# Folding wv and wo into one matrix, ordering the first loads by use, and running attention tiles across the two sequences

## The reference

```python
# 1: causal attention, one head of 128
q = rope(xn @ wq);  k = rope(xn @ wk);  v = xn @ wv
s = (q * 128**-0.5) @ (k * 128**-0.5).T - 1e30 * (i < j)
o = softmax(s) @ v
x = x + o @ wo
# 2: x = x + ffn(layernorm(x))           token shift, sigmoid gate, squared relu
# 3: x = x + linear_attention(layernorm(x))   16 heads of 64, a state per head, gated
# 4: x = x + ffn(layernorm(x))           the same weights as block 2
```

## Time and profile before

| | us |
|---|---|
| median of 3 runs | 904.65 (904.13 to 906.27) |
| the profiled execution | 908.08, its span 906.0 |
| busy PE / DVE / ACT / POOL over the span | 824.8 / 554.9 / 569.4 / 584.4 |

### The profile page before, as it was taken

How to read it: one execution, slowest core, us unless ns; L and a number is a source line. 1 busy time by engine, 2 the same in 40 slices (tenths; PEclk the granted TensorE clock), 3 DMA queues, 4 the chain that set the end, 5 groups by cost and what they waited for, 6 DMA issues and landing times.

```text
span 906.0 us, 31429 instructions
## 1 busy us (share of the span) xinstructions
PE 824.8 (91%) x13280; PEld 711.7 (79%) x13280; DVE 554.9 (61%) x1296; ACT 569.4 (63%) x1202; POOL 584.4 (65%) x514
## 2 busy tenths in 40 slices
PE   4858998999797799999999999999999999997877
PEld 3647997899695687888788788888888888885776
DVE  3976566567684356557467467467467467566473
ACT  4746554665565666767767767767767766754544
POOL 4983211320455788977977977977977977986322
PEclk9988999999997899999999999999999999997999
DMA  5001000100100000000000000000000000000011
GB/s 190 26 12 36 25 13 1 31 18 2 25 1 1 1 3 3 4 3 3 3 3 3 4 3 3 4 3 3 4 2 3 3 3 3 3 3 2 13 31 51
DMA packets 19417, 12.38 MB, mean 14 GB/s; under 512 B 7760, under 2 KB 18768, under 8 KB 19024
## 3 DMA queue, kind: packets, MB, share of 16 engines
q1 hardware_dynamic: 19280, 10.39, 4.0%
HBM read 8.29 MB, written 2.10 MB: 11 GB/s over the span
## 4 chain that ended last, share of the span: by engine, by line
PE 50%; DVE 9%; POOL 4%; issue 3%; ACT 2%; DVEq 0%; POOLq 0%; ACTq 0%
PE la_ps L1465 7%; PE la_ps L1467 6%; PE la_ps L1466 6%; DVE la_u_lo L1773 4%; PE la_o_ps L1528 4%; PE la_o_ps L1544 4%; PE la_s_ps L1558 4%; PE la_ps L1575 3%; PE la_ps L1509 3%; DVE la_u L1767 3%; PE la_ps L1609 2%; PE la_ps L1496 2%; PE la_ps L1610 2%; PE la_ps L1611 2%; PE la_ps L1598 1%
## 5 line engine op out<-in xcount | busy, mean ns | idle before, releaser
L2109 POOL TENSOR_TENSOR la_coef<-la_ssk,lt_mhalf 128x32 f32<-128x32 f32 x16 | 87.1, 5442 | 71.2 <-DVE la_ssk L1784 71.2
L1465 PE MATMUL la_ps<-la_x_hi,w_hi 128*128 128x256 f32 x384 | 116.7, 304 | 2.0 <-ACT la_v L1924 1.0
L1467 PE MATMUL la_ps<-la_x_hi,w_lo 128*128 128x256 f32 x384 | 107.6, 280 | 0.1
L1466 PE MATMUL la_ps<-la_x_lo,w_hi 128*128 128x256 f32 x384 | 107.5, 280 | 0.0
L2141 POOL TENSOR_TENSOR la_scale<-la_scale,lt_mhalf 128x32 f32<-128x32 f32 x16 | 99.9, 6241 | 6.7 <-DVE la_scale L1760 6.4
L1807 DVE TENSOR_TENSOR lt_state<-la_s_ps,la_faded 128x512 f32<-128x512 f32 x62 | 42.6, 687 | 70.6 <-PE la_o_ps L1544 57.5
L1465 PEld LDWEIGHTS la_ps<-la_x_hi,w_hi 128*128 128x128 f32 x384 | 72.4, 189 | 14.5 <-issue 6.2
L713 ACT ACTIVATE at_probs<-at_s_ps,at_ntop 128x512 f32<-128x512 f32 (+2 forms) x80 | 49.0, 623 | 46.5 <-DVE at_ntop L655 46.4
L598 PE MATMUL at_o_ps<-V,at_probsT 128*128 128x128 f32 x544 | 74.6, 277 | 3.2 <-DVE at_probsT L507 2.0
L531 POOL CAST at_q_hi<-qk_hi 128x128 fp32r<-128x128 f32 x32 | 9.4, 294 | 104.9 <-PE at_s_ps L572 102.4
L598 PEld LDWEIGHTS at_o_ps<-V,at_probsT 128*128 128x128 f32 x544 | 69.1, 192 | 6.5 <-ACT at_probsT L729 2.3
(11 more groups left out here) (216 smaller groups left out, 2501.3 us busy)
## 6 DMA issues: line engine op xcount, KB each, us to landing
at_w_raw<-in_w SPq DMA_DIRECT2D x20, 128.0 KB, 2.2
X<-in_x SPq DMA_DIRECT2D x8, 256.0 KB, 2.9
out<-X SPq DMA_DIRECT2D x8, 256.0 KB, 2.3
qkv_cos<-in_cos SPq DMA_DIRECT2D x1, 1024.0 KB, 5.0
qkv_sin<-in_sin SPq DMA_DIRECT2D x1, 1024.0 KB, 7.2
lt_w_out<-in_w_out SPq DMA_DIRECT2D x4, 128.0 KB, 2.7
const<-in_const SPq DMA_DIRECT2D x1, 320.5 KB, 3.3
qkv_w<-in_w_qkv SPq DMA_DIRECT2D x1, 320.0 KB, 3.9
```

Of the source, the lines that this page charges most:

```text
L1465: eng.matmul(out, l_hi, r_hi, start=True, stop=False)
L1466: eng.matmul(out, l_hi, r_lo, start=False, stop=False)
L1467: return eng.matmul(out, l_lo, r_hi, start=False, stop=True)
L2109: eng.tensor_tensor(coef[:, :], ssk[:, :], mhalf[:, :], ALU.pow).then_inc(s["coef_step"], 1)
```

## The change

It has three parts. First, `qkv_phase` loads wo, turns wv on TensorE, copies it, multiplies it by wo and copies the product `w_vo`, which then takes wv's place in `values`; attention loses `scale_o`, `turn_o`, `copy_oT` and `project_o`, and `residual` becomes one operation on VectorE that scales o out of PSUM by the inverse row sum and adds X. The ring of PSUM banks holds only probabilities. Second, the loads of the beginning stand in order of use: the constants are cut into the identity (early) and the rest (last), and the cosine and sine tables come in four pieces, each waited for by `products`; preparation of the FFN weights moves behind tile 4 of sequence 0. Third, the scores, maxima and exponentials of sequence 1's first tiles are issued in the iteration of sequence 0's last tile, and the waits count tiles on across the sequences.

```diff
...
+        wo = sb("wo", [P, P])
+        wvT = sb("wvT", [P, P])
+        w_vo = sb("w_vo", [P, P])
...
                 if k == 0:
-                    eng.dma_start(const[:, :], io["const"]).then_inc(loaded_const, 16)
                     eng.dma_start(w[:, :, :], io["w_qkv"]).then_inc(loaded_w, 16)
+                    eng.dma_start(ident, io["const"][:, C_IDENT:C_IDENT + P]).then_inc(loaded_ident, 16)
+                    eng.dma_start(wo[:, :], io["wo"]).then_inc(loaded_wo, 16)
 
                 eng.wait_ge(loaded_x, 16 * (k + 1))
-                if k == 1:
-                    eng.dma_start(cos[:, :], io["cos"]).then_inc(loaded_rope, 16)
-                    eng.dma_start(sin[:, :], io["sin"]).then_inc(loaded_rope, 16)
+                if g.b == 1:
+                    part = slice(g.n * G, (g.n + 1) * G)
+                    if g.n > 0:
+                        eng.wait_ge(loaded_rope, 32 * g.n)
+                    eng.dma_start(cos[:, part], io["cos"][:, part]).then_inc(loaded_rope, 16)
+                    eng.dma_start(sin[:, part], io["sin"][:, part]).then_inc(loaded_rope, 16)
+            eng.dma_start(const[:, P:], io["const"][:, P:]).then_inc(loaded_rest, 16)
+            eng.wait_ge(loaded_rest, 16)
...
             def products(g, r):
                 if late(g, 1):
                     eng.wait_ge(rot_ready[r], g.count(1))
+                eng.wait_ge(loaded_rope, 32 * (g.n + 1))
...
             moments(Tile(0, 1))
-            eng.wait_ge(loaded_rope, 32)
+            eng.wait_ge(wv_turned, 1)
+            eng.tensor_copy(wvT[:, :], pr_ps[0][:, 0:P]).then_inc(wvT_ready, 1)
+            eng.wait_ge(w_vo_full, 1)
+            eng.tensor_copy(w_vo[:, :], pr_ps[1][:, 0:P]).then_inc(w_vo_ready, 1)
             run_slots(eng, slot)
...
         @block.tensor
         def _(eng):
-            eng.wait_ge(loaded_const, 16)
+            eng.wait_ge(loaded_ident, 16)
             eng.wait_ge(loaded_w, 16)
+            eng.transpose(pr_ps[0][:, 0:P], w[:, 4, :], ident).then_inc(wv_turned, 1)
+            eng.wait_ge(loaded_wo, 16)
+            eng.wait_ge(wvT_ready, 1)
+            eng.matmul(pr_ps[1][:, 0:P], wvT[:, :], wo[:, :], start=True, stop=True).then_inc(w_vo_full, 1)
...
-                    mm = eng.matmul(v_ps[g.b][:, j * P:(j + 1) * P], xT[:, g.b, j * P:(j + 1) * P], w[:, 4, :], start=True, stop=True)
+                    mm = eng.matmul(v_ps[g.b][:, j * P:(j + 1) * P], xT[:, g.b, j * P:(j + 1) * P], w_vo[:, :], start=True, stop=True)
...
-        def ahead(n):
+        def ahead(b, n):
 
             if n + 2 < SMALL:
-                return n + 2
-            return n + 1 if SMALL <= n + 1 < NT else None
+                return [(b, n + 2)]
+            if n + 1 == NT and b + 1 < B:
+                return [(b + 1, 0), (b + 1, 1)]
+            return [(b, n + 1)] if SMALL <= n + 1 < NT else []
...
-        jobs = []
-        for n in range(NT + 2):
-            if n < NT:
-                jobs += [("probs", n, j) for j in range(blocks(n))]
-            if 1 <= n <= NT:
-                jobs.append(("oT", n - 1, 0))
-            if n >= 2:
-                jobs.append(("wo", n - 2, 0))
+        jobs = [("probs", n, j) for n in range(NT) for j in range(blocks(n))]
...
-            def turn_o(b, n):
-                eng.wait_ge(o_ready, b * NT + n + 1 + CREDIT)
-                bank, full = wait_bank(b, ("oT", n, 0))
-                eng.transpose(bank[:, 0:P], o_n[:, n % 2, :], ident).then_inc(full, 1)
-
-            def project_o(b, n):
...
-                eng.matmul(bank[:, 0:P], oT[:, n % 2, :], wo[:, :], start=True, stop=True).then_inc(full, 1)
-
+            scores(0, 0)
+            scores(0, 1)
             for b in range(B):
-                scores(b, 0)
-                scores(b, 1)
-                for n in range(NT + 2):
-                    last = blocks(n) if n < NT else 0
+                for n in range(NT):
+                    last = blocks(n)
                     for j in range(min(last, 2)):
                         transposes(b, n, j)
-                    if ahead(n) is not None:
-                        scores(b, ahead(n))
-                    for j in range(last - 1):
+                    for later in ahead(b, n):
+                        scores(*later)
+                    for j in range(last):
                         values(b, n, j)
                         if j + 2 < last:
                             transposes(b, n, j + 2)
-                    if 1 <= n <= NT:
-                        turn_o(b, n - 1)
-                    if n >= 2:
-                        project_o(b, n - 2)
-                    if n < NT:
-                        values(b, n, last - 1)
...
             def residual(b, n):
-                k, before = ring(b, ("wo", n, 0))
-                eng.wait_ge(t_full[k], before + 1)
-                xt = X[:, bass.ds(b * NT + n, 1), :]
-                eng.tensor_tensor(xt, t_ps[k][:, 0:P].rearrange("p (t c) -> p t c", t=1), xt, ALU.add).then_inc(t_read[k], 1)
+
+                N = b * NT + n
+                eng.wait_ge(o_full, N + 1)
+                eng.wait_ge(total_step, 2 * N + 2)
+                xt = X[:, b * NT + n, :]
+                eng.scalar_tensor_tensor(xt, o_ps[n % 2][:, 0:P], total[:, n % 2, 1:2], xt, ALU.mult, ALU.add).then_inc(o_read, 1)
...
+                for n in range(NT):
+                    if n > 0:
+                        residual(b, n - 1)
+                    elif b > 0:
+                        residual(b - 1, NT - 1)
+                    if n + 2 < SMALL:
                         sum_rows(b, n)
-                    if ahead(n) is not None:
-                        maxima(b, ahead(n))
-                    if n < NT and ahead(n) != n + 2:
+                    for later in ahead(b, n):
+                        maxima(*later)
+                    if n + 2 >= SMALL:
                         sum_rows(b, n)
-                    for j in range(2, last):
+                    for j in range(2, blocks(n)):
                         copy_probs(eng, eng.tensor_copy, b, n, j)
-                    if 1 <= n <= NT:
-                        copy_oT(b, n - 1)
-                    if n >= 2:
-                        residual(b, n - 2)
+                    if b == 0 and n == GT:
+                        ffn_weights.vector(eng)
...
-            def scale_o(b, n):
-                N = b * NT + n
...
-                eng.activation(o_n[:, n % 2, :], o_ps[n % 2][:, 0:P], ACT.Copy, scale=total[:, n % 2, 1:2]).then_inc(o_ready, 1)
-
             eng.sem_inc(exp_ready, CREDIT)
-            eng.sem_inc(o_ready, CREDIT)
-            ffn_weights.scalar(eng)
+            exponentials(0, 0)
...
                     if n + 1 < NT:
                         exponentials(b, n + 1)
-                    scale_o(b, n)
+                    elif b + 1 < B:
+                        exponentials(b + 1, 0)
+                    if b == 0 and n == GT:
+                        ffn_weights.scalar(eng)
             tables.scalar_rates(eng)
```

68 lines of the change are left out of this document (23 added, 45 removed).

## The result

The changed kernel takes 884.07 us (median of 4 runs, 882.93 to 884.72), the kernel before in the same series 905.46 (904.13 to 909.5). The ratio is 0.9738, with a 95% interval of 0.9709 to 0.9767. The forecast was 884.4. The profiled executions took 882.93 and 908.08 us, with spans of 880.8 and 906.0.

The account below looks back on a forecast made before the run. TensorE was taken to bound mid-sequence attention, chains of waits the opening, sequence step and end. Terms summed to 20.3 us off 908.08, giving 887.8, less 3.43 to the median: 884.4 us, own range 880 to 888.5, overall 879.5 to 892.

Parts of the forecast that it names:

- The opening: Kernel's start up to the first products: they come earlier because the wait for the sine table goes; 3.5 us, bounds 0 and 4.7.
- the three chains: Opening, paths to the first products: third X lands near 10.9, products possible at 13.9; weights' product and TensorE, 14.5; VectorE's second copy, hidden.
- The start: Start of attention: the first mask no longer waits behind the FFN weights' preparation; 1.7 us, up to 2.0.
- The -0.3: Tile 4 of sequence 0: cost of the FFN weights' six instructions moved there; -0.3 us, bounds 0 and -1.1.
- my two readings of the clock: Start of attention: full clock returns at a fixed moment, gain 1.0 us, or earlier work brings it earlier, gain 2.0 us.
- TensorE's work on o, and the ring: Attention tiles: turn and wo product removed, 8.2 us, bounds 5 and 9.5; PSUM banks no longer wait for o's copies, 1.3.
- the first rival: Small attention tiles: VectorE and ScalarE take over, TensorE's saving pays only in tiles 9 to 15; 892.9 us, chance 0.13.
- Between the sequences: Step from sequence 0 to 1: the next sequence's first scores and exponentials lie under the last tile; 3.2 us, bounds 1.5 and 3.9.
- the end: End of attention: last values, projection and residual behind VectorE's FFN groups get shorter; 2.7 us, bounds 1.5 and 3.2.
- The opening gave more than nothing: Second rival, opening: it gives nothing because GpSimd and VectorE are full or a load is late again; 887.9 us, chance 0.10.
- The loads one behind another: Third rival, opening: SP's waits between X and table pieces make the kernel slower; 907.4 us, chance 0.03.
- My sign of being wrong: Stages after attention: one changing its length by more than 2 us would count against the forecast.

Follow-up runs that it names:

- w_late: The changed kernel with the FFN weights' preparation in tile 12 of sequence 0 instead of tile 4; median 884.92 us, attention 0.38 us shorter.
- u_weights: The changed kernel with the FFN weights' preparation back at the head of VectorE's and ScalarE's streams; median 885.41 us, attention 0.40 us longer.
- the pair put back: The changed kernel with one turn and one 128x128 product more per tile on TensorE, into unread PSUM columns; median 894.39 us, attention 6.2 us longer.
- fold_only: The kernel before with only wv and wo multiplied on chip, no projection of o, and the residual in one operation; median 894.91 us, ratio 0.9873.
- loads_only: The kernel before with only the new order of the loads, without the product of the weights; median 903.53 us, ratio 0.996.

## Why the prediction was right, step by step

**The opening** (3.5; 3.0 at the first products, 3.9 at the first scores). Right in the main cause, the wait for the tables. Of the three chains the one through the product and TensorE was the last, as said: `products` wait 0.67 us for TensorE. The third X landed at 11.41, 0.5 later than worked out. It was issued at 7.32, behind 0.33 + 0.43 us in which SP issues the two pieces, where I had started from 6.7. (The prediction's second estimate, 3.8 us, is worked out from a fit to DMAs that GpSimd issues; SyncE issues these, and from its own issue this one took 4.1.) The products were 0.4 later than forecast, but not for that: I had left out group 0's values, which TensorE makes from 10.98 for 2.04 us ahead of group 1's turn and projections. Before, they lay in the wait for the tables (10.06 to 12.13). By the Trainium skill, "DMA: Bandwidth & Descriptors", section "Bandwidth", loads under 1 MiB are the worse ones; whole tables under the same waits were slower by 3.7 us, so here what is queued ahead of X decided. That the new product is nearly free holds only with the new loads: under the old ones it costs 3.1 us, which no part of the prediction had.

**The start** (1.7; 1.92). The first mask came as early as said, but this term was mis-sized: 1.7 - 0.3 = 1.4 was counted, and undoing the step costs 0.40 by the end of attention. The -0.3 was about right (`w_late` gives 0.38 back), so the 1.7 was worth 0.8. The full clock returned at 68.90 instead of 73.51, 4.6 us earlier, but not because the start of attention was freed: in `u_weights`, where TensorE again stands 2.46 us behind its first scores, it returned at 68.61. What moved with it is the fall to half clock, while TensorE stands behind its last projections: 63.27 before, 58.66 after, 58.37 in `u_weights`. Between fall and return lie 10.2 us in all three. So of my two readings of the clock the fixed moment is the one borne out for this step; it moved with the end of the stage before, not with the start of attention. The other reading, which I took from the Trainium skill, "TensorE: Matmul & The Clock Gate", section "Part 1: The HAM clock gate", that the earlier work brings the clock earlier, isn't borne out by this pair. How much of the missing 0.9 us is the clock's and how much other chains' in the small tiles was not separated.

**TensorE's work on o, and the ring** (8.2 + 1.3; with the weights 9.2 for the tiles, 9.47 measured). The sum came out right, the split was wrong, and its two errors offset each other: that is luck. I multiplied 23 tiles by 0.336 us and left out tile 8 alone. The leads of the masks say where it pays: tiles 4 to 8 give 5.72, 6.46, 7.27, 7.26, 8.50, which is 0.7 a tile, twice what TensorE works on o (with the fold alone it is 0.9 a tile, in both sequences); tiles 8 to 15 give 8.50, 8.51, 8.62, 8.73, 9.00, 9.28, 9.83, 10.06, 0.22 a tile. (The turns in the earlier trace rows are tile 8's, not tile 9's as I wrote.) What the gain is lost to in tile 9 is in TensorE's timelines, first before, then after: turns of eight blocks of tile 9, of the last two, and of the first eight of tile 10.

```profile
101.21 1.06 PE L584 MATMUL at_t_ps<-const,at_probs 128*128 128x128 f32 x8
...
104.92 0.38 PE L584 MATMUL at_t_ps<-const,at_probs 128*128 128x128 f32 x2
...
106.81 1.04 PE L584 MATMUL at_t_ps<-const,at_probs 128*128 128x128 f32 x8
```
```profile
92.21 1.32 PE L594 MATMUL at_t_ps<-const,at_probs 128*128 128x128 f32 x8
...
96.30 0.38 PE L594 MATMUL at_t_ps<-const,at_probs 128*128 128x128 f32 x2
...
97.90 1.04 PE L594 MATMUL at_t_ps<-const,at_probs 128*128 128x128 f32 x8
```

Before, 101.21 to 106.81 is 5.60 us; after, 92.21 to 97.90 is 5.69. The second part is shorter (1.89 to 1.60) by the work on o that left. The first part is longer (3.71 to 4.09), of which 0.26 are the turns, which now last 1.32 instead of 1.06. ScalarE's timeline after shows why: the second exponential of tile 9 is still running when the turns have begun, and ends at 92.73.

```profile
92.05 0.68 ACT L699 ACTIVATE at_probs<-at_s_ps,at_ntop 128x512 f32<-128x512 f32 x1
```

So the probabilities of tile 9 come late as well. This is the first rival's mechanism, in tiles 8 and 9 instead of in all small tiles. TensorE counts as busy 48.00 of 48.02 us over it, since such a wait lies inside an instruction's length and in no idle.

In the small tiles it is the other way round: more than the work was saved. The fold took 15.4 us off attention. Of that TensorE's own time is 6.2 to 7.2 (the pair put back), ScalarE's 0.1, VectorE's 0.5. What is left, near 8, should be waits of the removed chain itself (values, scaling, turn, copy, projection, residual, and two more turns in the ring of banks), which no engine's time shows. Where it lies, `fold_only` set against the kernel before tells, by the masks and less what the pair costs in the same place: 2.5 us in tiles 0 to 8 of sequence 0, 1.6 in tiles 2 to 8 of sequence 1, 0.6 in tiles 8 to 15 of both, 1.8 from tile 15 of sequence 0 to tile 2 of sequence 1, 2.3 at the end, and 0.4 ahead of the first mask. These 9.2 us include what ScalarE and VectorE took. The trace shows one such wait named, 1.6 us in the earlier trace rows. That the rest is waits of this chain is reached by difference and was not tested, because a chain can't be put back without its work.

**Between the sequences** (3.2; 3.89) and **the end** (2.7; 2.70). Right. The step has two parts that I had not told apart: the run-on is worth 2.1 (1.9 without the scatter ahead of it), the fold 1.8 to 2.0. At the end VectorE holds to its own order as said, and the residual cost 0.35 instead of 0.29. TensorE's idle there fell from 1.99 to 1.60 us, where I had let it grow.

**The rivals.** VectorE and ScalarE taking over would have given 892.9: a pair of tiles, not the stretch, was due to them. The opening gave more than nothing. The loads one behind another never were late: no `products` waited for a table. My sign of being wrong, a later stage changed by more than 2 us, did show (3.3), but kernels with the change lie on both sides of it. The last step, from the profiled execution to the median (-3.43), held by luck: the profiled execution after lies 1.1 below its median, not 3.4 above. Between the profiled executions lie 25.2 us where I said 20.3; the later stages' 3.3 and the ledger's 1.6 too many make that up, and in the medians 21.4 were left.

## What to carry to other kernels

Work taken off a busy engine is worth its time only in the stretches where that engine's stream is never late; look for instructions that last longer than their like (1.32 us against 1.04), for a busy share near 100% hides them. A serial chain over three engines is worth more than the sum of its work wherever tiles are short or the stream starts and ends: here 15.4 us for some 7 of engine time. And an edit that puts one small wait into an in-order stream (the product of the weights) is free or costs 3 us by what stands ahead of the wait, so it is to be timed together with the loads.

## What the runs showed of the hardware beyond that

- VectorE's scaling and adding out of PSUM, 128 x 128, takes 0.34 to 0.35 us; the plain addition took 0.28 to 0.29.
- VectorE's operation over 128 x 4 takes 0.16 us alone and 1.22 us at 9.23, where GpSimd's 128 x 512 operation runs from 9.17 for 1.26; in the earlier trace rows it is 1.24 and 1.28, and 1.27 in `loads_only` at 14.39. The long ones end when GpSimd's operation does (10.45 and 10.43; 15.66 and 15.64): the two engines don't run independently there.
- TensorE's granted clock fell to half (1.2 GHz) while it stood between its last projections and the first scores, and the stretch at half clock lasted 10.2 us in twelve of the fourteen traces, whether TensorE stood 2.9 us behind its first scores (before) or 0.9 (after). It lasted 6.8 us with the pair put back (61.13 to 67.95) and 13.7 with the loads alone (58.06 to 71.71). What made the two exceptions was not tested.
- Openings of equal code scatter by 1.0 us, the later stages by 6 (with 26 to 38 us of them at half clock), both more than several of the effects sought here. The lead measured inside one stage of the traces separated what the medians didn't.
